# A new order for the third chunk's layers, the last four tiles and the end, with four half-wide slots for layer 1

## The reference

```python
e = stack([tbl_f[ids[:, f]] for f in range(26)], axis=1)    # 2048 x 26 x 128, float32
sd = einsum('bfd,bd->bf', e, dense)                          # dense is 2048 x 128
ss = einsum('bfd,bgd->bfg', e, e)
pairs = ss[:, iu, ju]                                        # the 325 pairs above the diagonal
h = concatenate([dense, sd, pairs, dense], axis=1)           # 2048 x 607
h = maximum(h @ W_top1 + b_top1, 0)                          # 607 -> 512
h = maximum(h @ W_top2 + b_top2, 0)                          # 512 -> 256
y = h @ W_top3                                               # 256 -> 1
```

## Time and profile before

| | |
|---|---|
| median of three runs | 381.33 us |
| the profiled execution's own time | 381.86 us |
| its span (first to last instruction) | 380.1 us |
| busy: PE, POOL, DVE, ACT | 347.9, 266.8, 253.0, 186.8 us |
| gathers on POOL | 272, mean 0.978 us, 0.30 us between two |
| mean granted TensorE clock | 0.978 of full speed |

### The profile page before, as it was taken

The page is one execution under the profiler, slowest core; times in us unless marked ns, Lnnn a source line. Parts: engine busy times, 40 slices in busy tenths (PEclk is TensorE's granted clock), DMA queues, the critical chain, the costliest instruction groups (busy, mean ns, idle before and its releaser), DMA issues.

```text
span 380.1 us, 12743 instructions
## 1 busy us (share of the span) xinstructions
PE 347.9 (92%) x5585; PEld 273.3 (72%) x5585; DVE 253.0 (67%) x502; ACT 186.8 (49%) x319; POOL 266.8 (70%) x279
## 2 busy tenths in 40 slices
PE   2899988998799998999999999998999999778896
PEld 0566666886588887786788877886688877568785
DVE  0799899985788634886888635885888634625341
ACT  3366677676223335767224335676224335534352
POOL 5777778777777777777777777777777777777000
PEclk9999999999999998999999998999999998969999
DMA  7998114333322321333332331333233121221000
GB/s 192 261 251 191 50 48 105 93 98 106 89 79 83 82 86 50 90 89 106 95 87 76 85 90 50 91 102 104 81 88 82 49 64 50 54 57 50 13 3 0
DMA packets 20112, 33.43 MB, mean 88 GB/s; under 512 B 7918, under 2 KB 10492, under 8 KB 20058
## 3 DMA queue, kind: packets, MB, share of 16 engines
q0 software_dynamic: 8704, 17.84, 18.6%
q1 hardware_dynamic: 11353, 14.78, 14.3%
HBM read 32.60 MB, written 0.01 MB: 86 GB/s over the span
## 4 chain that ended last, share of the span: by engine, by line
PE 40%; POOL 37%; issue 15%; DVE 4%; DMA 2%; ACT 2%; POOLq 0%; SPq 0%; DVEq 0%
POOL rows L527 37%; PE late_bank L551 8%; PE late_bank L552 7%; PE late_bank L636 5%; PE gram_bank L591 4%; PE turn_bank L572 3%; PE spare_bank L802 2%; PE spare_bank L551 2%; PE spare_bank L680 1%; DMA rows<-in_tbl_dram,index 1%; PE spare_bank L552 1%; PE gram_bank L551 1%; PE gram_bank L552 1%; DVE one_hot L1016 1%; DVE one_hot L1018 1%
## 5 line engine op out<-in xcount | busy, mean ns | idle before, releaser
L527 POOL DMA_INDIRECT rows<-in_tbl_dram,index x272 | 266.0, 978 | 84.4 <-issue 81.1
L1018 DVE TENSOR_TENSOR one_hot<-table_ids,row_number 125x512 fp32r<-125x512 int32 x216 | 134.3, 681 | 27.9 <-PE gram_bank L552 14.5
L378 ACT COPY turned<-turn_bank 128x512 f32<-128x512 f32 (+1 forms) x68 | 67.6, 1033 | 46.9 <-PE turn_bank L572 46.9
L551 PE MATMUL late_bank<-one_hot,table_hi 125*128 125x512 f32 x168 | 71.7, 427 | 1.9 <-DVE one_hot L1016 1.0
L552 PE MATMUL late_bank<-one_hot,table_lo 125*128 125x512 f32 x168 | 67.5, 402 | 0.0
L591 PEld LDWEIGHTS gram_bank<-turned 128*27 128x27 f32 x4096 | 45.1, 107 | 20.1 <-issue 17.3
L591 PE MATMUL gram_bank<-turned 128*27 128x26 f32 x4096 | 54.1, 195 | 4.3 <-issue 2.5
L572 PE MATMUL turn_bank<-ident,rows 128*128 128x128 f32 x288 | 46.9, 289 | 10.3 <-DMA rows<-in_tbl_dram,index 6.0
L572 PEld LDWEIGHTS turn_bank<-ident,rows 128*128 128x128 f32 x288 | 36.0, 148 | 21.0 <-DMA rows<-in_tbl_dram,index 10.0
L551 PEld LDWEIGHTS late_bank<-one_hot,table_hi 125*128 125x128 f32 x168 | 32.3, 192 | 16.3 <-issue 5.3
L1016 DVE TENSOR_SCALAR one_hot<-looked_up,row_number_sb 125x512 fp32r<-125x512 f32 x72 | 33.6, 506 | 11.5 <-issue 6.1
(11 more groups left out here) (121 smaller groups left out, 457.9 us busy)
## 6 DMA issues: line engine op xcount, KB each, us to landing
table_ids<-in_ids_by_table_dram SPq DMA_DIRECT2D x27, 256.0 KB, 3.3
rows<-in_tbl_dram,index POOLq DMA_INDIRECT x272
turned<-in_tbl_dram SPq DMA_DIRECT2D x6, 448.0 KB, 12.1
looked_up<-in_tbl_dram SPq DMA_DIRECT2D x3, 448.0 KB, 6.1
rows<-in_r_dense_features_dram SPq DMA_DIRECT2D x16, 64.0 KB
gram<-in_W_top_dram SPq DMA_DIRECT2D x1, 702.0 KB
gram<-in_W_top_dram SPq DMA_DIRECT2D x1, 512.0 KB
turned<-in_tbl_dram SPq DMA_DIRECT2D x6, 52.0 KB
```

The source lines that it names most:

```text
L378: copy(to[:, f0:f1], of).then_inc(rows_copied[n % 2], 1)
L527: pool.indirect_dma_start(out=rows[:, row % RING_ROWS, :], out_offset=None, in_=tables[f], in_offset=bass.IndirectOffsetOnAxis(ap=index[:, ...
L551: pe.matmul(bank, table_hi[:, s, k, :], hot, start=k == 0, stop=False)
L1018: last = nc.vector.tensor_tensor(hot, table_ids[0:RK, (chunk.n * LOOKUPS + s) % ID_SLOTS, 0:wide], row_number[0:RK, k:k + 1].broadcast_to( ...
```

## The change

The change does four things.

- **The third chunk's layers** (part CLOSING, tiles 8 to 11) leave `work_off` after their `dense_ahead`. They are written out in `work_off_last` between the turns, the products and the last look-ups of tiles 12 and 13, on PE, ACT and DVE alike. Layer 2 of CLOSING gets the banks `spare_bank` and `row_number`, and `h2` lies at the other end of its room.
- **The chunks' borders**: `layer3` of a chunk runs after the first products of the next one (`first_products`), and the last look-ups of a chunk run after the turns of the next one's first tile. Layer 2 of a whole chunk makes its two halves in the other order.
- **The end**: the turns of tile 15's row groups stand later in PE's list. Tile 15's group g0 is turned after EARLY's `turn_products`; g3 comes after all of EARLY's layer 1, and g4 directly before EARLY's last layer 2 piece. FINAL's `dense_ahead` runs for three n, all before tile 15's last products.
- **Slots and banks**: half-wide parts use the two slots of `h1_hi` and `h1_lo` as four. FINAL's layer 1 has four banks, and so neither `relu1` nor `layer1` waits for a slot or a bank there.

```diff
+        def h1_bank(part, n):
+            return (final_h1_bank if part is FINAL else shared_h1_bank)[n][:, 0:width(part)]
+        def h1_slot(h1, part, n):
+            if part.tiles == TILES:
+                return h1[:, n % H1_SLOTS, :]
+            return h1[:, n // 2, n % 2 * width(part):(n % 2 + 1) * width(part)]
+        def dense_parts_ahead(part):
+            return 3 if part is FINAL else 2
...
             def layer1(part, n):
-                if n >= 2:
+                if n >= 2 and part is not FINAL:
                     pe.wait_ge(h1_split, part.n * N1 + n - 1)
-                for k in range(int(n < 2), K1):
+                for k in range(int(n < dense_parts_ahead(part)), K1):
...
             def half_layer3(part):
+                if part is EARLY:
+                    wait_all_rows(pe, tiles * TURNS)
...
+            def first_products(chunk):
+                turn_rows(chunk, 1, turns_before(0))
+                if chunk.n > 0:
+                    pe.wait_ge(h2_made, (chunk.n + 1) * N2)
+                products(chunk, 0, 0)
+                if chunk.n > 0:
+                    layer3(CHUNKS[chunk.n - 1])
...
             def work_off_last():     # PE
-                for t in range(HALF):
-                    for u in range(UNITS):
-                        turn_rows(LAST, t + 1, turns_before(u))
-                        products(LAST, t, u)
...
-                turn_rows(LAST, 3, (0,))
+                layer1(CLOSING, 0)
+                look_up(LAST, blocks_after("layer1", 0))
+                look_up(LAST, blocks_after("layer1", 1))
+                turn_rows(LAST, 0, (0,))
+                layer1(CLOSING, 1)
...
+                layer2(CLOSING, 2)
+                turn_rows(LAST, 2, (0, 1))
+                products(LAST, 1, 0)
+                layer2(CLOSING, 3)
+                turn_rows(LAST, 2, (2,))
+                products(LAST, 1, 1)
+                layer3(CLOSING)
...
                 dense_ahead(EARLY, 0)
                 for g in range(COLS_TURNS):
                     turn_products(EARLY, g)
+                turn_rows(LAST, 3, (0,))
...
             def relu1(part, n):      # ACT
-                if n >= H1_SLOTS:
+                if n >= H1_SLOTS and part.tiles == TILES:
                     act.wait_ge(h1_used, part.n * (N1 - 1) + n - H1_SLOTS + 1)
...
             def work_off_last():     # DVE
-                copy_rows(dve, LAST, 3, (1,))
+                split_h1(EARLY, 0)
                 place_found(dve, LAST, 3)
-                split_h1(EARLY, 0)
+                copy_rows(dve, LAST, 3, (1,))
```

More of the change, by code:

```diff
@@ L327, in h2_bank @@
         def h2_bank(part, n):
+            if part is CLOSING:
+                return closing_h2_bank[n]
             return (whole_h2_bank if part.tiles == TILES else half_h2_bank)[n][:, 0:width(part)]
@@ L333, in h2_of, with h2_order @@
             return h2[:, n] if part.tiles == TILES else half_h2[:, n]
+        def h2_order(part):
+            return range(N2 - 1, -1, -1) if part.tiles == TILES else range(N2)
         def copy_products(engine, chunk, n):
@@ L611, in turn_products @@
                         pe.wait_ge(y_rows_copied, 1)
+                    if g == 2 and part is FINAL:
+                        pe.wait_ge(y_copied, EARLY.n + 2)
                     if g >= COLS_TURNS - 2:
@@ L784, in work_off_last @@
                     turn_pairs(FINAL, k)
-                dense_ahead(FINAL, 1)
                 for n in range(N1):
@@ L915, in work_off_last @@
-                copy_rows(act, LAST, 3, (0,))
+                relu1(CLOSING, 0)
+                copy_found(LAST, blocks_after("layer1", 1))
+                copy_rows(act, LAST, 0, (0,))
+                relu1(CLOSING, 1)
+                copy_rows(act, LAST, 0, (1, 2))
+                copy_found(LAST, blocks_after("layer1", 3))
+                copy_rows(act, LAST, 0, (4,))
+                copy_rows(act, LAST, 1, (0,))
+                relu1(CLOSING, 2)
+                copy_rows(act, LAST, 1, (2,))
@@ new lines, in work_off_last @@
+                copy_products(act, LAST, 1)
+                place_found(act, LAST, 1)
+                relu1(CLOSING, 3)
+                copy_rows(act, LAST, 1, (4,))
+                copy_products(act, LAST, 3)
+                copy_rows(act, LAST, 2, (0,))
+                for i in range(N2):
+                    relu2(CLOSING, i)
+                copy_rows(act, LAST, 2, (2,))
+                copy_products(act, LAST, UNITS + 1)
+                copy_output(CLOSING)
+                copy_rows(act, LAST, 2, (4,))
@@ L920, in work_off_last @@
                 copy_products(act, LAST, 2 * UNITS + 1)
[L921 removed]
+                for n in range(N1 - 1):
+                    relu1(EARLY, n)
                 copy_rows(act, LAST, 3, (2,))
[L923 to L924 removed]
                 copy_products(act, LAST, 2 * UNITS + 3)
[L926 removed]
+                relu1(EARLY, N1 - 1)
                 copy_rows(act, LAST, 3, (4,))
+                for i in range(N2):
+                    relu2(EARLY, i)
                 copy_products(act, LAST, 3 * UNITS + 1)
[L929 to L930 removed]
                 copy_output(EARLY)
```

180 lines of the change are left out of this document (114 added, 66 removed).

## The result

The changed kernel takes 377.93 us (median of 6 runs, 377.65 to 378.32), the kernel before 381.41 us beside it (6 runs, 380.28 to 382.24): ratio 0.991, 95% interval 0.989 to 0.993, so the gain of 0.9% is small but clear of the noise. The forecast was 378.0 us. On another chip the changed kernel was timed again against before, with ratio 0.988 (0.987 to 0.990). The profiled execution took 378.13 us. Ratios are of the chip's usual state; two executions further down that fell in its slower state (one of `before_pad` at 390.19 us, one of the kernel before beside it) are left out of them.

The account below looks back on a forecast made before the run. POOL's gathers set the pace, their last landing at 353.45 us fixed, then FINAL's chain on PE. Terms 1.5 + 0.55 + 1.3 = 3.35 us off the median 381.33 gave 377.9, stated as 378.0 us; range 377.0 to 379.0.

Parts of the forecast that it names:

- (1): CLOSING's layers mixed among tiles 12 and 13: worth 0, bounds 0 and 2 us late.
- (2): EARLY's columns ahead of tile 15's g0: EARLY starts 3.1 us earlier, PE just in time for g3 and g4.
- Rival (b): PE late at the last landing, g4's turn about 1 to 1.5 us late: 379.2 us; chance 0.19.
- (3): Last group, g4 of tile 15: its turn follows the landing directly, so its products start 1.5 us earlier.
- (4): From the last group's first products to FINAL's `turn_products`: 0.55 us less, the gap among the products kept at 1.0.
- Rival (a): No gap in tile 15's products, blocks of instructions falling elsewhere or loading hidden: 1.0 us better, 376.9 us; chance 0.14.
- (5): FINAL's layers after `turn_products`: dense piece gone, fewer layer 1 matmuls, `relu1` with its own slot; together 1.3 us.
- (c): Rival: a new wait in ACT's or DVE's list holds the last products, cancelling 3 us: 381.0 us; chance 0.09.
- (d): Rival: PE's clock falls again after 351 us, adding 5.5 us: 383.4 us; chance 0.06.

Follow-up runs that it names:

- before_pad: The kernel before, with 128 idle semaphore increments at the head of PE's list: 386.83 us, ratio 1.011.
- g0_first: The changed kernel, with the turn of tile 15's g0 and its ACT copy back ahead of EARLY's columns: 380.53 us, ratio 0.9953.
- no_mix: The changed kernel, with CLOSING's layers in one piece again and tiles 12 and 13 behind them: 378.14 us, ratio 0.990.
- slot_wait: The changed kernel, with FINAL's `relu1` of n = 2 and 3 waiting for layer 2 as if there were two slots: 378.73 us, ratio 0.9922.
- the second profile: The changed kernel unedited, run again as the control on the last chip: 378.45 us, ratio 0.9883.
- after_dve64: The changed kernel, with 64 idle semaphore increments on VectorE, eight in each of tiles 2 to 9: 377.51 us, ratio 0.9876.
- half3_behind: The changed kernel, with `half_layer3(EARLY)` behind the products of tile 15's last piece, likewise on ACT: 378.69 us, ratio 0.9911.

## Why the prediction came out right, and where it was off

*What bounds the kernel.* Right: POOL's last gather stayed (350.92 and 350.65), and the time follows from the last landing plus the end's chain in every run but two: in `g0_first` and `before_pad` PE came to g4's turn 2.75 and 4.45 us behind the landing.

*(1) The mixing, 0.* Right (`no_mix`). The check behind it was 3.5 us off: PE reached tile 14's g2 at 324.64, not 321.1, 2.1 us behind its landing (the last gather started at 319.99). Of the 3.5 us, 2.2 came from ahead of the mixed list, which the prediction had put at 0: PE had waited 3.57 us for a gather at 265.07 us (1.16 at 263.98 in before), with the granted clock at 0.50 behind it, and came to CLOSING's layer 1 2.2 us later than in before (290.58 against 288.42). Two further waits (0.91 and 1.21 us at 328.69 and 331.23) took it all up, as the prediction said they would.

*(2) EARLY earlier by 3.1 us.* Right: 332.96 against 332.9 forecast. PE came to g3 at 351.65, where the sum gave 350.75. The clock explains most of it. It stood at 0.50 for 6.8 us in both, from 331.8 to 338.6 in before and from 330.0 to 336.8 after, but EARLY's stretch began earlier within it. So 3.9 us of the stretch ran at the lower level instead of 2.6, which costs some 0.65 us by estimate (half of the 1.3 us more). The prediction had kept that share as it was. The windows that give these ends, first of before and then of after:

```profile
336.00:338.00 2.00, 2.00 (x11) 1.84 (x10) 0.04 (x1) 1.10 (x1) 1.39 (x3) 0.50 0.12 33
```

```profile
336.00:338.00 2.00, 2.00 (x17) 1.86 (x16) 1.03 (x8) 0.81 (x7) 1.53 (x2) 0.79 0.22 55
```

Rival (b) was thus true in kind, with 0.17 us at g4 in place of 1 to 1.5. Where the clock stayed up or came back sooner (`slot_wait`, `no_mix`, the second profile), PE waited 0.66 to 0.78 us for g4.

*(3) The last group, 1.5 us.* The stretch from the landing to the first products shrank by 1.38 to 1.40. In `g0_first` the first products start at 356.46, in before at 356.21, so that with g0 ahead again all of this term is gone.

*(4) The products, 0.55 us.* 1.2 us in the first profile and 0.69 in the second. The gap was kept at 1.0 us, and it measured 0.15 and 0.67: this is the term that was mis-sized. Without the gap the stretch is 4.92 us in before, 4.58 and 4.57 after, so the work gave 0.35 of the 0.55 that were forecast, since the dense piece that came in took 0.55 us (355.21 to 355.76) and not 0.35. The shorter gap gave 0.86 and 0.34 on top. Rival (a), no gap at all, was half true, and for its first reason: the block's end fell at another place, and the block before it, with layer 1, `half_layer3` and products in it, takes 2.75 us instead of 2.3. That is worth about 0.45 us; the rest of the 0.86 is chance, for 0.15 us is the shortest gap of the nine profiles with these products.

*(5) FINAL's layers, 1.3 us.* 0.74 and 0.77. From layer 2's first pair to `half_layer3` the stretch went from 7.13 to 6.09 us, 1.04 where 0.35 + 0.7 had been forecast; the slots hold 0.7 of it (`slot_wait`). The error is in the part ahead, 0.2 us gained by the forecast: it lost 0.30 (7.74 to 8.04). 0.37 of this is the hold at a block's end on VectorE (`after_dve64`). VectorE's list has two instructions fewer ahead of the first split in the changed kernel, and this put the block's end there; no row of the kernel before had it there.

So the sum of 3.35 us met the measured 3.33 of the first profile by luck: step (4) gave 0.65 us more than forecast and step (5) 0.56 less, and the causes, the gap and the hold on VectorE, have nothing to do with each other. The second profile, with a gap of 0.67, stands at 2.86 us. What was right for its own reasons is the fixed landing, the 3.1 us at EARLY, the last group and the slots.

*(c) and (d)* didn't happen. No copy was late for a product. The clock was 1.00 from 340 to 370 us, though idle times of up to 1.41 us stood in this stretch over the runs; only behind the 2.18 us of `before_pad` did it fall, in that one profile. One reading of rows under (d) was wrong: the fall at 332 us in before did not follow the 2.64 us of idle time. That began at 332.66, and the clock was at 0.50 from 331.8 on, behind 0.90 and 0.59 us. The Trainium skill's page "TensorE: Matmul & The Clock Gate", section "HAM oscillation — how this bites in real kernels", has it fall in short bursts between waits for DMA. The fall at 330 us in the changed kernel, between waits of 0.91 and 1.21 us for gathers, agrees with it. The fall in `before_pad` came in dense products, with no such wait.

*Still open:* why the same list of instructions gives a gap of 0.15 us once and of 0.67 another time. The packet came 0.7 and 0.85 us after PE entered the block and the resumption 2.2 and 2.6 us after the packet, so the time of the fetch itself varies; what it depends on was not tried. Nor was a cut in the count of small products, which would lengthen every block, nor the chunks' borders, the four banks and the third dense piece by themselves. Why the late packet of `before_pad` came when it did is open as well.

## What to carry to other kernels

Where gathers on one queue set the pace, compare variants by stretches from the last landing to the end: a median of 380 us hides the 0.35 and 0.7 us that such a stretch shows to a few hundredths. Where an engine is no longer on time for the landing, compare times from the start instead. Put work that waits for a landing behind work that is ready. In a run of small matmuls count the instructions per block: where a block of 128 pairs was used up in less than the 2.9 to 3.7 us seen here, the engine stood at its end, and an edit far ahead moved the place of it. When a sum comes out to the hundredth, check it term by term: here two wrong terms cancelled.

## What the hardware showed that I had not expected

- A fetch of instructions is on the path of a dense stretch of TensorE: 0.15 to 2.18 us at a block's end. All 19 gaps between products in 13 profiles stand at the same place in a block of 256 instructions, and the place shifts by exactly 64 pairs for 128 idle instructions.
- VectorE shows a hold of 0.37 us at an end of its blocks of 8 KB, though no packet was due there.
- The clock fell once, to 0.50, behind 2.18 us without work amid dense products (`before_pad`); behind 1.41 us (`half3_behind`) and less it stayed at 1.00.
- An increment of a semaphore isn't free: the records of the 128 at the head of a list stand 0.15 us apart on TensorE, whose first matmul moved from 3.86 to 20.50 us, and 0.09 us apart on VectorE, whose first instruction moved from 3.02 to 13.34 us.
